# Norms clamped from PSUM and GpSimd's routing constants moved, in a scan-attention and mixture-of-experts kernel

## The reference, cut to what matters

```python
q = _l2norm((x @ Wq).reshape(b, s, nh, d))       # nh = 16 heads of d = 8
k = _l2norm((x @ Wk).reshape(b, s, nh, d))       # _l2norm: a / max(sqrt(sum(a*a)), 1e-12)
v = (x @ Wv).reshape(b, s, nh, d)
beta = sigmoid(x @ Wbeta)
def step(state, inp):                            # over the 2048 rows
    kk = kt[..., :, None] * kt[..., None, :]
    state = state * (1.0 - bb * kk) + bb * (vt[..., :, None] * kt[..., None, :])
    out_t = einsum('bhij,bhj->bhi', state, qt)
out = layer norm of out, * ln_g + ln_b
out = out * silu(x @ Wg); return out @ Wout
```

## Time and profile before

| | |
|---|---|
| three runs | 509.23, 507.26, 508.70 us |
| span of the profiled execution | 505.8 us (its own time outside the span is not recorded) |
| TensorE | 434.7 us busy, 86% |
| VectorE | 299.7 us busy, 59% |
| ScalarE | 228.6 us busy, 45% |
| GpSimd | 257.2 us busy, 51% |
| scan stage | about 17.7 to 122 us of the span |

### The profile page before, as it was taken

One profiled execution on the slowest core, in us unless ns is written; L12 is line 12 of the kernel. 1 busy time (PEld: TensorE's weight loads), 2 busy tenths in 40 slices (PEclk: granted clock), 3 DMA queues, 4 the chain that ended last, 5 costly groups with the idle time before them and its releaser, 6 DMA issues.

```text
span 505.8 us, 7932 instructions
## 1 busy us (share of the span) xinstructions
PE 434.7 (86%) x2766; PEld 302.8 (60%) x2766; DVE 299.7 (59%) x712; ACT 228.6 (45%) x351; POOL 257.2 (51%) x321
## 2 busy tenths in 40 slices
PE   7887695868778899999989999888966989999980
PEld 6534252425677778888965333335545967888860
DVE  4899899998520313215696999899954201211354
ACT  4867673433110352242167998876842013224220
POOL 5897785898648854565340000022546533455470
PEclk9999996978979999999999999999987899999996
DMA  5455473991342211225613434594011121221266
GB/s 136 141 196 209 143 256 98 330 280 38 75 163 68 74 60 55 78 58 192 189 42 95 99 95 101 143 277 154 28 37 43 38 79 42 63 76 55 73 228 209
DMA packets 50327, 60.87 MB, mean 120 GB/s; under 512 B 7152, under 2 KB 29296, under 8 KB 50288
## 3 DMA queue, kind: packets, MB, share of 16 engines
q1 hardware_dynamic: 42672, 47.50, 31.8%
q0 software_dynamic: 4608, 8.47, 5.2%
q10 hardware_dynamic: 3008, 4.40, 2.7%
HBM read 29.78 MB, written 25.31 MB: 109 GB/s over the span
## 4 chain that ended last, share of the span: by engine, by line
PE 30%; issue 20%; SPq 15%; DMA 6%; DVE 4%; POOL 1%; another core or an unknown queue 1%; ACT 1%; POOLq 0%; ACTq 0%; DVEq 0%
PE ps L1354 26%; SPq L390 12%; SPq L322 3%; PE ps L1510 2%; DMA chosen_y<-ye,y_to 2%; DMA last_got<-chosen_y 1%; DMA got<-chosen_y 1%; PE ps L1358 1%; POOL chosen_y L552 1%; DMA xe<-slots_x 1%; DVE xn L1249 1%; DMA slots_x<-rows_x,put_at 0%; DVE stats L1238 0%; DVE xres L1178 0%
## 5 line engine op out<-in xcount | busy, mean ns | idle before, releaser
L552 POOL DMA_INDIRECT chosen_y<-ye,y_to x80 | 78.8, 985 | 77.0 <-DVE ye L1224 56.1
L729 ACT ACTIVATE hT<-ps 128x640 f32<-128x640 f32 x64 | 45.1, 704 | 86.2 <-issue 53.3
L502 POOL DMA_INDIRECT slots_x<-rows_x,put_at x64 | 62.9, 982 | 41.3 <-issue 19.4
L1358 PE MATMUL ps<-ident 128*128 128x128 f32 x576 | 75.7, 293 | 5.6 <-POOL head_of L423 2.1
L1278 DVE SCALAR_TENSOR_TENSOR feat<-expo,ps 128x1024 f32<-128x1024 f32 x64 | 76.4, 1217 | 3.7 <-ACT expo L858 3.3
L858 ACT ACTIVATE expo<-ps,minus_one 128x1024 f32<-128x1024 f32 x64 | 70.4, 1116 | 12.9 <-PE ps L1354 9.0
L1358 PEld LDWEIGHTS ps<-ident 128*128 128x128 f32 x576 | 70.5, 152 | 8.5 <-issue 3.7
L1354 PE MATMUL ps<-cproj_sb,hT 128*128 128x128 f32 x640 | 74.6, 275 | 0.3
L1354 PEld LDWEIGHTS ps<-cproj_sb,hT 128*128 128x128 f32 x640 | 73.0, 192 | 0.9 <-issue 0.6
L1354 PE MATMUL ps<-xeT,cfc_sb 128*128 128x320 f32 x256 | 71.7, 433 | 2.1 <-DVE xeT L1189 2.1
L1189 DVE COPY xeT<-ps 128x640 f32<-128x640 f32 x16 | 13.2, 825 | 93.6 <-PE ps L1510 46.3
(11 more groups left out here) (230 smaller groups left out, 603.7 us busy)
## 6 DMA issues: line engine op xcount, KB each, us to landing
chosen_y<-empty_rows SPq DMA_DIRECT2D x32, 256.0 KB
decay<-k_rows SPq DMA_DIRECT2D x30, 256.0 KB, 5.4
stk<-part SPq DMA_DIRECT2D x96, 64.0 KB, 2.0
slots_x<-empty_rows SPq DMA_DIRECT2D x16, 325.0 KB, 6.3
xe<-slots_x SPq DMA_DIRECT2D x16, 325.0 KB
cfc_sb<-in_L_ffn_c_fc SPq DMA_DIRECT2D x2, 2048.0 KB
got<-chosen_y SPq DMA_DIRECT2D x8, 256.0 KB
got<-chosen_y ACTq DMA_DIRECT2D x8, 256.0 KB
```

Of the source, the lines that this page charges most:

```text
L502: pool.indirect_dma_start(out=slots_x[k], out_offset=bass.IndirectOffsetOnAxis(ap=put_at[:, c, kk, t:t + 1], axis=0), in_=rows_x[:, kk * N ...
L552: pool.indirect_dma_start(out=chosen_y[k], out_offset=bass.IndirectOffsetOnAxis(ap=y_to[:, b, i:i + 1], axis=0), in_=ye[:, b, i * D:(i + 1 ...
L729: act.activation(hT[:, b, f, :].rearrange("p (a n) -> p a n", a=2), ps[:, 2 + 2 * (f % 2):4 + 2 * (f % 2), 0:HALF], ACT.Gelu).then_inc(h_r ...
L1358: pe.transpose(ps[:, bank, 0:P], ident[:], ident[:])
```

## The change

ScalarE's square root of a whole block's norms is written back into bank 7 instead of into `norm` in SBUF, and VectorE's clamp reads it from there. The half-block forms are as before. TensorE's `turn_o` of blocks 0 and 1, which overwrites the bank, waits for the clamp instead of the root. On GpSimd the constants of the routing, the iota with them, stand behind `empty_rows` and behind the eight normed rows, instead of in front of both. No other wait is changed.

```diff
+            pool.memset(empty_rows[:, :, 0:D], 0.0)
+            pool.memset(empty_rows[:, :, D + 1:ROW], 0.0)
+            pool.memset(empty_rows[:, :, D:D + 1].bitcast(I32), int(FAR)).then_inc(zeroed, 1)
+            pool.wait_ge(ln_rstd[0], NB)
+            for t in range(2 * TB, NT):
+                pool.tensor_scalar(xn[:, t, :], xres[:, t, :], mv[:, t, 0:1], rstd[:, t:t + 1],
+                                   ALU.subtract, ALU.mult).then_inc(xn_late, 1)
             for e in range(NE):
                 pool.memset(base_share[:, 0, e:e + 1], float(NS * e))
                 pool.memset(base_share[:, 3, e:e + 1], float(NS * (e + 1)))
...
             pool.memset(minus_one[:], -1.0)
             pool.iota(rows_x[:, :, D].bitcast(I32).rearrange("p (c s) -> p c s", s=TB), [[BK, KT // TB], [1, TB]], base=0,
                       channel_multiplier=TB).then_inc(ids_made, 1)
-            pool.memset(empty_rows[:, :, 0:D], 0.0)
-            pool.memset(empty_rows[:, :, D + 1:ROW], 0.0)
-            pool.memset(empty_rows[:, :, D:D + 1].bitcast(I32), int(FAR)).then_inc(zeroed, 1)
-            pool.wait_ge(ln_rstd[0], NB)
-            for t in range(2 * TB, NT):
-                pool.tensor_scalar(xn[:, t, :], xres[:, t, :], mv[:, t, 0:1], rstd[:, t:t + 1],
-                                   ALU.subtract, ALU.mult).then_inc(xn_late, 1)
...
             def norms(c):
                 act.wait_ge(sumsq_mm, part_done(c, 1))
-                act.activation(flat(norm[:]), ps[:, 7, 0:TB * 2 * H], ACT.Sqrt).then_inc(norm_ready, 1)
+                act.activation(ps[:, 7, 0:TB * 2 * H], ps[:, 7, 0:TB * 2 * H], ACT.Sqrt).then_inc(norm_ready, 1)
...
             def clamp(c):
                 dve.wait_ge(norm_ready, part_done(c, 1))
                 dve.wait_ge(wide_ready, 2 * c)
-                dve.tensor_scalar(rnorm[:], norm[:], 1e-12, None, ALU.max).then_inc(rn_clamped, 1)
+                dve.tensor_scalar(flat(rnorm[:]), ps[:, 7, 0:TB * 2 * H], 1e-12, None, ALU.max).then_inc(rn_clamped, 1)
...
             def turn_o(c):
                 pe.wait_ge(oT_ready, c + 1)
                 if c + 2 < NB:
-                    pe.wait_ge(norm_ready, part_done(c + 2, 1))
+                    pe.wait_ge(rn_clamped, part_done(c + 2, 1))
```

## The result

| | before | after |
|---|---|---|
| median of 5 runs | 509.23 us (507.26 to 510.6) | 515.2 us (512.68 to 515.7) |
| span of the profiled execution | 505.8 us | 514.0 us |
| ratio of the times | | 1.0092, 95% interval 1.0065 to 1.012 |

The kernel became slower by 4.7 us by the ratio (the two medians of the table stand 6.0 apart), where a gain of 0.6 us was forecast and the range ended at 512.0. The profiled execution is the longest of the five (515.7 us), and that of before (505.8 us of span) lies at the low end of its own. What lies behind that scan differs by up to 3.8 us between profiles of one program: 386.0, 387.9, 387.6 and 384.1 us in the four of the kernel before.

A forecast was written before the change was run, and what follows sets the result against it. VectorE was taken to bound the kernel from about 17.7 to 122 us. Terms 3.6 + 1.4 - 5.6 = -0.6 us on a 505.8 us span, with 2.9 us from span to time, gave 508.1 us; range 506.0 to 512.0.

The forecast's parts named there:

- Step 4: GpSimd's constants moved behind the normed rows: 0 us on GpSimd, VectorE stands 3.6 us before its scan loop for the iota.
- Step 5: Half-block clamps from SBUF, shifted later against GpSimd's products: together +1.4 us, bounds -0.3 to +5.7.
- The slower rival: Early half clamp at 23.85 us shut out by GpSimd, chance 0.30; missing all changes: 6.0 us wait, sum +3.7, 512.4.
- Steps 2 and 3: ScalarE's root written in place in PSUM, 0 us (-0.1 to +0.1, twice); TensorE's `turn_o` waiting for the clamp, 0 us.
- Step 1: VectorE's whole-block clamps of blocks 2 and 3, read from PSUM: gain 4.87 + 0.72 = 5.6 us, bounds 0 to 5.9.
- The 2.9 us: Distance of the three runs' median, 508.7 us, above the profiled span of 505.8, taken as fixed.
- the block exclusion: VectorE two-port and GpSimd instructions exclude each other; by this alone block 2's clamp gains at most 1.2 us.
- Stall taken up elsewhere: Rival: the stall at VectorE's loop head is absorbed, the 5.6 us gain remains, 503.1 us; chance 0.06.
- the clamp from PSUM waits as well: Rival: the PSUM clamp brings little or nothing, so 3.6 + 1.4 = +5.0 us, 513.7 us; chance 0.04.

The follow-up runs named there:

- e2: GpSimd's new order alone on the kernel before, root and clamp still through SBUF: 513.76 us, ratio 1.0079.
- e4: The changed kernel with 36 unread transposes of the identity keeping TensorE busy during VectorE's stall: 510.56 us, ratio 1.0035.
- e1: The kernel before with only the whole-block clamp from PSUM, GpSimd's program as before: 507.48 us against 509.5, ratio 0.9956.
- e3: The changed kernel with VectorE's wait for the iota moved to its first use in the routing: 508.42 us, ratio 0.9984.
- e8: e1 plus transposes keeping TensorE busy in two waits and the weights' transposes moved later: 506.23 us against 509.6, ratio 0.9943.
- e9: The kernel before, unchanged, profiled a third time: single time 510.35 us.

## Why the prediction was wrong, point by point

**Step 4, the stall: right.** VectorE stood 3.53 us, 3.6 predicted, released by the iota. The rows of x began at 13.70, and GpSimd's decay products were not held by the constants but by a DMA (0.30 us).

**Step 5, the half clamps: right in kind, sized too large.** Against the first profile of before they cost 0.3 + 0.6 - 0.3 = 0.65 us, 1.4 predicted. But there, too, the prediction had read one draw: the three halves took 0.80 us together in that profile, 1.22, 1.38 and 1.28 in the three others, and 1.45 in the changed kernel. Against those three the new place costs 0.1 to 0.2 us. The slower rival, a half shut out for 6 us, did not come.

**Steps 2 and 3: right.** The root in place takes 0.26 us; `turn_o` is not held.

**Step 1, the clamp: the step that failed.** "The gain is 4.87 + 0.72 = 5.6 us", on a path where "one taken off brings it forward". The local size was right for that profile: between scans 8 and 9 the changed kernel gains 6.49 - 1.43 = 5.06 us. Two things were wrong in putting it on the path. First, 5.16 us was one draw of several: 5.16, 1.26, 1.26 and 3.86 in four profiles, and 1.26 in the new order (e2). Second, most of it does not reach the end. At scans 10, 11, 15, 17 and 18 the changed kernel gives back 1.34 + 1.45 + 0.79 + 0.77 + 0.23 = 4.6 us of its 5.1. The profiles of before with a short clamp give back 3.3 to 3.8 of 3.9. Of the 1.8 us at scans 15 to 18, e4, with the same clamp, gives back only 0.6, so not all of that is the clamp's. The waits of the earlier trace rows showed VectorE waiting for almost nothing, but that was read from an execution in which VectorE had been delayed by 5 us and the others had run ahead. That a wait is absent says who was last in that run, not by how much. What stays is of the size of two short clamps, 1.26 + 0.93 us, made 0.27 + 0.29: 1.6 us. e1's last scan stands 1.1 to 1.3 us ahead of the first, second and fourth profile of before, and its time is 2.2 us lower (0.9 to 3.6 by the interval). Beside the new order nothing of it is seen (e2).

**A term that the sum did not have: the clock.** The prediction counted what queues behind the stalled VectorE on VectorE, and not what TensorE does meanwhile. It stood 4.58 us, its clock fell to 0.50, and the waits that follow put 0.5 us on scan 2 and 1.8 us on scan 5. e4 keeps TensorE busy, and VectorE's waits for it fall by 2.3 us; by the times it gets back 2.9 us. Of the two falls only the first stands right behind the stall. The second, behind the wait of 1.27 us, is also in e3, e8 and e9, which have no stall, and not in e2, which has it and whose first fall is longer; its price in this profile is the stall's only in part, if at all. How often either comes is known from one profile for each kernel and four of the kernel before.

**The sum again, with what was measured,** at the scans of the changed kernel against the first profile of before: stall and half clamps 3.6 + 0.65; TensorE's late v +2.3; clamp -5.1; handed back +4.6; at the last scan, another wait for TensorE of 0.4; together 6.5 us, with 4.7 by the times. The 2.9 us that the prediction put between span and time are in part a fast execution: wherever the record has both, the time is 1.7 to 1.8 us above the span. Of the prediction's views, the block exclusion is the one where the Trainium skill was weighed (SBUF — State Buffer, Who interferes with whom): the loser is blocked until the other instruction has finished. Two of the four profiles agree, with 1.26 us beside one instruction of 1.27; in the two others the clamp missed three and four changes, so here the rule gives the wait when the clamp gets in at the first change, and not the wait.

**Rivals.** "Stall taken up elsewhere" is excluded by e2, "the clamp from PSUM waits as well" by sixteen clamps of 0.27 to 0.29 us in the changed kernel, e1 and e3 to e8. None of the rivals was the one that came. That last rival's +5.0 us lies next to the 4.7 measured, but by luck, as its cause is not there.

## What to carry to other kernels

When a constant is moved behind other work on its engine, look for every wait on its signal, and move the wait to the first use along with it; e3 shows that one line was worth the whole loss. A stall on the engine that leads can cost more than its length when TensorE stands behind it, as it did here: look up what TensorE has to do there and what it would take at half clock. And before a long wait in one profile is counted as a gain, profile the same kernel again, and ask what the other engines did in that time.

## What the runs showed of the hardware that was not expected

A VectorE operation between two SBUF tiles can miss one change of GpSimd's instruction after another until GpSimd stops: it took 5.16, 1.26, 1.26 and 3.86 us at the same place of the same program. GpSimd's own instructions were lengthened by 0.03 us at most. TensorE's clock at one place, too, differs between executions: behind the same wait of 1.27 us it fell in one of four profiles of the kernel before, and the products behind took 3.67 us instead of 1.98. The times go with it. Of the 34 runs of the kernel before that stand beside e1 to e4, the ten with a mean granted clock of 0.938 or more took 508.2 us on average, the fifteen with 0.930 or less 510.4. Which of the two brings the other is not shown by this.
